# Mixer's front: ScalarE normalises the first chunk, VectorE evicts its turned blocks, TensorE multiplies the identity with itself 20 times beforehand

## The chip, the cores and the metric

The program runs on one core of one Trainium2 chip. The metric is device microseconds of one execution. The kernel before was timed three times: median 945.87 us, from 944.41 to 945.95 us.

## What is computed

The input is `x`, 2 sequences of 2048 tokens with 128 features. Four stages follow each other, each with a layer norm ahead of it and its result added to `x`: a Mamba mixer, a mixture of 8 experts, a linear attention, and the same mixture of experts again. The change is in the first stage alone:

```
xn = layernorm(x)                       # over the 128 features, eps 1e-5
x_m, z = split(xn @ W_in)               # 256 channels each
x_m = silu(conv(x_m, 4 taps) + conv_b)
dt_low, Bc, Cc = split(x_m @ W_x)
dt = softplus(dt_low @ W_dt + b_dt)
state[t] = exp(dt * A) * state[t-1] + dt * Bc * x_m     # 16 states a channel
y = (sum(state * Cc) + x_m * D) * silu(z)
x = x + y @ W_out
```

Then `x + moe(layernorm(x))`, `x + attention(layernorm(x))` and `x + moe(layernorm(x))`.

## The kernel before

Everything is float32. The mixer (`mamba`, from line 36) keeps the 4096 tokens in `X` as 32 tiles of 128 tokens by 128 features. Eight tiles are a chunk, so there are four chunks; four tiles fill a PSUM bank of 512 columns when they are turned.

Each engine has a program of its own, and semaphores order them. The front, which the change touches, goes like this for chunk 0:

- SyncE (lines 244 to 259) issues the four loads of `X`, then seven loads that count on one semaphore, `w_loaded`: `w_x`, `w_dt`, `w_out`, `decay_rate` and three small vectors into `chan`, `b_dt` last. ScalarE's queue issues three more weights (lines 328 to 331).
- VectorE takes the statistics of a chunk (`token_stats`, line 452, with lines 28, 31 and 457), ScalarE the square root (`std`, line 337), VectorE the reciprocal and the shift (lines 464 and 466), and then VectorE normalises the 8 tiles into `xn` (line 471). `xn` is a view of the tile `decay`, so the trace names it `decay`. The statistics of chunks 1 to 3 and the normalisation of their 24 tiles come behind that in VectorE's program.
- TensorE turns the tiles (`turn`, line 578; a bank is ready when `turned` counts), and ScalarE copies bank 0 and bank 1 into `xn_T` (`take_turned`, line 341), which counts on `xnT_ready`.
- GpSimd makes the convolution's weights meanwhile: `w_tap` (line 283, 4 multiplications), then the copy of `pick` into `pick_r` (line 286), then `skip` (line 290), which waits for all of `w_loaded`.
- TensorE then waits for `taps_ready`, for all of `w_loaded` (line 673) and for two banks of `xn_T` (line 682). Its pieces `u` (line 623) are four matmuls each, one for each tap, 512 columns wide. The order written out in `START` (line 209) is: two `u` pieces of the first half of the chunk, bank 2 turned (chunk 1's first four tiles), two `u` pieces of the second half, the `mixed` pieces (line 634), `bT`, `v`, then banks 3 to 7 turned, `again`. ScalarE evicts the `u` pieces with Silu (line 350) and bank 2 (line 341).

After the front there is a loop of 128 steps (16 states, 2 channel blocks, 4 chunks): ScalarE makes the decay (line 432), VectorE the drive (line 538) and the scan (line 555), GpSimd the product with C (line 323), TensorE sums the products (line 702). A step of the loop cannot begin before the front has made `dt` and `u` of chunk 0, and the stages behind the mixer begin when the loop has ended.

Of the kernel before, what the change touches and what calls it, by code (L numbers as in the profile page):

```python
# [16 lines left out]
ACT = mybir.ActivationFunctionType  # L17
ALU = mybir.AluOpType

P = 128  # L20
BANK = 512
# [3 lines left out]
def layer_norm_constants(dve, chain, at, stats, moments, source, tiles):  # L25

    for i in range(tiles):
        dve.bn_stats(stats[:, i, :], source(i)).then_inc(chain, 1)
    dve.wait_ge(chain, at + tiles)
    for i in range(tiles):  # L30
        dve.bn_aggr(moments[:, i, :], stats[:, i, :]).then_inc(chain, 1)
    dve.wait_ge(chain, at + 2 * tiles)
    return at + 2 * tiles

def mamba(nc, X, ident, x, W_in, conv_w, conv_b, A_log, D, W_x, W_dt, b_dt, W_out):

    BATCH, L, DM = x.shape
    KC, _, CH = conv_w.shape
    NS = A_log.shape[1]  # L40
    R = W_dt.shape[0]
# [4 lines left out]
    CT = CHUNK // P  # L46
    TB = CHUNK // BANK
    BT = BANK // P
    RING = 4
    CHUNKS = BATCH * NCHUNK  # L50
# [8 lines left out]
    with nc.cleanup_on_exit(), ExitStack() as ctx:  # L59
        def sb(name, shape, dt=F32):  # L60
            return ctx.enter_context(nc.sbuf_tensor(name, shape, dt))

        def sem(name):
            return nc.alloc_semaphore(name)

        psum = ctx.enter_context(nc.psum_tensor("m_psum", [P, 8, BANK], F32))
        Y, DRIVE, PIECE = 0, 2, 6
# [13 lines left out]
        rstd = sb("m_rstd", [P, BATCH * TILES])  # L81
        shift = sb("m_shift", [P, BATCH * TILES])
        xn_T = sb("xn_T", [P, BATCH * L])
# [19 lines left out]
        xn = decay[:].rearrange("p r (t d) -> p (r t) d", d=DM)  # L103
# [14 lines left out]
        dve_chain = sem("m_dve_chain")  # L118
        variance = sem("variance")
        std_done = sem("std_done")  # L120
        normed = sem("normed")
        turned = sem("turned")
        xnT_ready = sem("xnT_ready")
# [108 lines left out]
        def place(n):  # L232
            h, s = divmod(n, NS)
            return h // KB, h % KB, s
# [92 lines left out]
        def _(act):  # L327
# [5 lines left out]
            def std(first, end):  # L333

                act.wait_ge(variance, end)
                part = rstd[:, first * CT:end * CT]
                act.activation(part, part, ACT.Sqrt).then_inc(std_done, 1)

            def take_turned(g):
                act.wait_ge(turned, g + 1)  # L340
                act.copy(xn_T[:, g * BANK:(g + 1) * BANK], psum[:, g % 4, :]).then_inc(xnT_ready, 1)  # L341
# [63 lines left out]
                             psum[:, Y + t, :]).then_inc(y_taken, 1)  # L405

            std(0, 1)
            take_turned(0)
            take_turned(1)
            std(1, CHUNKS)  # L410
            act.wait_ge(w_loaded, 16 * 7)
            for number, piece in enumerate(START):
# [7 lines left out]
            for n in range(STEPS):  # L420
                g, k, s = place(n)
# [3 lines left out]
                if before >= 0:  # L425
                    act.wait_ge(scanned, before + 1)
                    was, was_k, was_s = place(before)
                    if starts_batch(was):
# [4 lines left out]
                               scale=decay_rate[:, k, s:s + 1]).then_inc(decay_ready, 1)  # L433
# [15 lines left out]
        def _(dve):  # L449
            at = 0  # L450

            def token_stats(g, at):
                dve.wait_ge(x_loaded[g], 16)
                tiles = slice(g * CT, (g + 1) * CT)
                at = layer_norm_constants(dve, dve_chain, at, stats[:, tiles, :], moments[:, tiles, :],
                                          lambda i: X[:, g * CT + i, :], CT)
                dve.tensor_scalar(rstd[:, tiles], moments[:, tiles, 1], LN_EPS, None,
                                  ALU.add).then_inc(variance, 1)
                return at

            def normalise(first, end, at):
                tiles = slice(first * CT, end * CT)
                dve.wait_ge(std_done, 2 if first else 1)
                dve.reciprocal(rstd[:, tiles], rstd[:, tiles]).then_inc(dve_chain, 1)
                dve.wait_ge(dve_chain, at + 1)
                dve.scalar_tensor_tensor(out=shift[:, tiles], in0=moments[:, tiles, 0], scalar=-1.0,
                                         in1=rstd[:, tiles], op0=ALU.mult,
                                         op1=ALU.mult).then_inc(dve_chain, 1)
                dve.wait_ge(dve_chain, at + 2)
                for i in range(first * CT, end * CT):  # L470
                    dve.tensor_scalar(xn[:, i, :], X[:, i, :], rstd[:, i:i + 1], shift[:, i:i + 1],
                                      ALU.mult, ALU.add).then_inc(normed, 1)
                return at + 2

            at = normalise(0, 1, token_stats(0, at))
            for g in range(1, CHUNKS):
                at = token_stats(g, at)
            at = normalise(1, CHUNKS, at)
            dve.wait_ge(w_loaded, 16 * 7)  # L480
            dve.wait_ge(constants, 1)
            for k in range(KB):
# [36 lines left out]
            for number, piece in enumerate(START):  # L519
                if piece[:4] == ("again", 0, 0, 0):  # L520
                    dve.wait_ge(rate_exp, 1)
                    dve.tensor_scalar(decay_rate[:], decay_rate[:], -1.0, None,
                                      ALU.mult).then_inc(rate_ready, 1)
                    for g in range(TB + 1, BATCH * L // BANK):
                        dve.wait_ge(turned, g + 1)
                        dve.tensor_copy(xn_T[:, g * BANK:(g + 1) * BANK],
                                        psum[:, g % 4, :]).then_inc(xnT_ready, 1)
                use(piece, number)
            dve.wait_ge(dt_ready, TB)
            dve.wait_ge(u_ready, KB * TB)  # L530
# [41 lines left out]
        def _(pe):  # L572
            def turn(g):
                if g >= 4:
                    pe.wait_ge(xnT_ready, g - 3)
                for i in range(4):
                    pe.wait_ge(normed, 4 * g + i + 1)
                    last = pe.transpose(psum[:, g % 4, i * P:(i + 1) * P], xn[:, 4 * g + i, :], ident[:])
                last.then_inc(turned, 1)
# [28 lines left out]
            def unit(piece, number, i):  # L608
# [51 lines left out]
                elif kind == "out":  # L660
# [6 lines left out]
                                             start=(c == 0), stop=(c == KB - 1))  # L667
                    last.then_inc(projected, 1)

            for g in range(TB):  # L670
                turn(g)
            pe.wait_ge(taps_ready, KC)
            pe.wait_ge(w_loaded, 16 * 7)
            for number, piece in enumerate(START):
                kind, _, k, t, _ = piece
                if (kind, k, t) == ("u", 0, 1):
                    turn(TB)
                if (kind, t) == ("again", 0):
                    for g in range(TB + 1, BATCH * L // BANK):
                        turn(g)  # L680
                if kind == "u":
                    pe.wait_ge(xnT_ready, t + 2)
                if kind == "mixed":
                    pe.wait_ge(w_all_ready, 1)
                    pe.wait_ge(constants, 5)
                for i in range(KC if kind == "u" else KB if kind == "mixed" else 1):
                    unit(piece, number, i)
# [21 lines left out]
            for n in range(STEPS + LAG):  # L709
                g, k, s = place(n)  # L710
                if n < STEPS:
# [4 lines left out]
                    if maker(n) == "dve":  # L716
                        for t in range(TB):
                            last = pe.matmul(pair(n)[:, t, :], pick_r[B_AT:P, s, :],  # L718
                                             b_split[B_AT:P, g % 2, t * BANK:(t + 1) * BANK],
                                             start=True, stop=True)  # L720
# [869 lines left out]
def build(nc, inputs, out):  # L1590

    mixer = {k[len("L0_attn_a_"):]: v for k, v in inputs.items() if k.startswith("L0_attn_a_")}
    linear = {k[len("L0_attn_b_"):]: v for k, v in inputs.items() if k.startswith("L0_attn_b_")}
    experts = {k[len("L0_ffn_"):]: v for k, v in inputs.items() if k.startswith("L0_ffn_")}
    BATCH, L, DM = mixer["x"].shape
    T = BATCH * L
    between = nc.dram_tensor("between", [T, DM], F32, kind="Internal").ap()
    with ExitStack() as ctx:
        X = ctx.enter_context(nc.sbuf_tensor("X", [P, T // P, DM], F32))
        ident = ctx.enter_context(nc.sbuf_tensor("ident", [P, P], F32))  # L1600
        identity(nc, ident)
        mamba(nc, X, ident, **mixer)

        E, FF, _ = experts["fc1s"].shape
        shared = {name: ctx.enter_context(nc.sbuf_tensor(f"shared_{name}", shape, F32))
                  for name, shape in (("gamma", [P, 2]), ("b1_T", [P, E * FF // P]),
                                      ("b2_all", [P, E, DM]), ("gate_pad", [P, P + P // E - 1]),
                                      ("w1_T", [P, E, FF]), ("w2_T", [P, E, FF // P, DM]))}
        moe(nc, X, ident, shared, "f1", between, True, **experts)
        attention(nc, X, ident, between, **linear)  # L1610
        moe(nc, X, ident, shared, "f2", out.rearrange("b l d -> (b l) d"), False, **experts)
# [26 lines left out]
```

## Time and profile before

| | us |
|---|---|
| median of three timed runs | 945.87 |
| lowest, highest | 944.41, 945.95 |
| span of the profiled execution, first to last instruction | 955.9 |
| VectorE busy, share of the span | 652.0, 68% |
| TensorE busy, share of the span | 683.2, 71% |

The profiled execution has a span that is 10.0 us longer than the median of the timed runs; of that execution no other time is known. So a stretch read from the trace is about one per cent longer than in a timed run, if what the profiler adds is spread evenly, which the trace doesn't tell. Times in the trace count from the first instruction. A group in the timeline is a run of instructions of one kind: its start, and the time from that start to the end of the last of them.

### The profile page before, as it was taken

Reading aid. Unit: us, or ns where it says so; the run is one execution under the profiler, and the core shown is the slowest. Engines: PE = TensorE matmul, PEld = TensorE weight load, DVE = VectorE, ACT = ScalarE, POOL = GpSimd, SP = SyncE. Lnnn points to the kernel's source line nnn. Section 1 sums busy time; section 2 is a strip of 40 time slices with the busy share of each in tenths; the row PEclk is TensorE's granted clock in tenths of the full one; section 3 lists DMA queues with packets and bytes.
Section 4 is the critical chain, followed back from the end, with each engine's and each line's share of the span. In section 5 each row is a group of like instructions: output and inputs, shape, how many; then the busy total and the mean of one; then the engine's idle time right before and its main releaser. Section 6 shows DMA issues by size and latency. Waiting matters only on the chain. (4 is left out here: it accounts for less than half of the span.)

```text
span 955.9 us, 11388 instructions
## 1 busy us (share of the span) xinstructions
PE 683.2 (71%) x3643; PEld 487.6 (51%) x3643; DVE 652.0 (68%) x1169; ACT 527.3 (55%) x987; POOL 529.8 (55%) x417
## 2 busy tenths in 40 slices
PE   4868987889887898988876575669550952277951
PEld 1445555665556655666655453546340841255631
DVE  6598889988898969899999598623112698832210
ACT  1569998579985989867984266023210446012320
POOL 5047657675667755576768330458861041176874
PEclk9978998889997899779889675589875876568976
DMA  5134343444344334443544360413334005122332
GB/s 134 62 117 149 134 137 134 152 135 132 133 136 154 134 132 137 149 135 133 171 139 132 94 194 13 110 35 41 41 29 102 1 1 154 31 53 30 42 34 22
DMA packets 59751, 95.55 MB, mean 100 GB/s; under 512 B 6344, under 2 KB 39920, under 8 KB 59696
## 3 DMA queue, kind: packets, MB, share of 16 engines
q1 hardware_dynamic: 47872, 85.15, 27.7%
q0 software_dynamic: 11264, 8.66, 7.2%
q10 hardware_dynamic: 560, 1.05, 0.4%
q8 instruction: 29, 0.48, 0.2%
q14 instruction: 26, 0.21, 0.1%
HBM read 81.73 MB, written 13.11 MB: 99 GB/s over the span
## 5 line engine op out<-in xcount | busy, mean ns | idle before, releaser
L323 POOL TENSOR_TENSOR product<-state,c_all 128x1024 f32<-128x1024 f32 x128 | 302.0, 2371 | 192.2 <-DVE state L555 177.9
L555 DVE TENSOR_TENSOR_SCAN state<-decay,m_psum 128x1024 f32<-128x1024 f32 x64 | 145.2, 2281 | 14.2 <-PE m_psum L728 5.6
L555 DVE TENSOR_TENSOR_SCAN state<-decay,carry,m_psum 128x1024 f32<-128x1024 f32 x64 | 148.7, 2340 | 7.5 <-PE m_psum L728 3.6
L702 PE MATMUL m_psum<-ident,product 128*128 128x128 f32 x1024 | 151.3, 296 | 3.3 <-POOL product L323 3.3
L1058 ACT ACTIVATE f_f_T<-f_psum,shared_b_T 128x512 f32<-128x512 f32 x64 | 44.0, 688 | 188.6 <-PE f_psum L1368 166.8
L432 ACT ACTIVATE decay<-dt,decay_rate 128x1024 f32<-128x1024 f32 x128 | 145.3, 1144 | 2.8 <-DVE state L555 2.4
L702 PEld LDWEIGHTS m_psum<-ident,product 128*128 128x128 f32 x1024 | 125.6, 153 | 33.8 <-issue 26.2
L389 ACT ACTIVATE drive_T<-dtu_T,b_T 128x128 f32<-128x128 f32 x384 | 121.7, 389 | 15.1 <-PE m_psum L728 13.7
L800 POOL DMA_INDIRECT f_got<-f_table,f_tokens x64 | 66.1, 1032 | 99.8 <-DMA f_table<-f_rows 41.4
L538 DVE TENSOR_TENSOR m_psum<-m_psum,dtu 128x1024 f32<-128x1024 f32 x80 | 97.3, 1217 | 26.4 <-PE m_psum L718 26.0
L718 PE MATMUL m_psum<-b_split,pick_r 64*128 64x512 f32 x160 | 64.2, 483 | 26.4 <-DVE state L555 26.1
L1353 PE MATMUL f_psum<-shared_w_T,f_f_T 128*128 128x128 f32 x512 | 66.9, 294 | 13.9 <-issue 7.5
L1353 PEld LDWEIGHTS f_psum<-shared_w_T,f_f_T 128*128 128x128 f32 x512 | 64.6, 208 | 19.3 <-issue 17.9
L1368 PE MATMUL f_psum<-f_y_T,shared_w_T 128*128 128x512 f32 x128 | 64.4, 650 | 7.9 <-DVE f_y_T L1224 7.9
L1224 DVE TENSOR_SCALAR f_y_T<-f_psum,shared_gamma 128x512 f32<-128x512 f32 x16 | 13.0, 810 | 81.9 <-PE f_psum L1342 65.3
L623 PE MATMUL m_psum<-xn_T,w_tap 128*128 128x512 f32 (+2 forms) x128 | 66.2, 647 | 1.6 <-ACT xn_T L341 1.6
L1000 POOL DMA_INDIRECT between<-f_f,f_tokens x32 | 50.4, 1576 | 21.4 <-issue 8.8
L1000 POOL DMA_INDIRECT out<-f_f,f_tokens x32 | 50.3, 1573 | 20.6 <-DVE f_f L1243 9.5
L728 PE MATMUL m_psum<-ident,drive_T 128*128 128x128 f32 x384 | 58.3, 302 | 3.7 <-DVE state L555 3.0
L728 PEld LDWEIGHTS m_psum<-ident,drive_T 128*128 128x128 f32 x384 | 50.5, 158 | 17.2 <-issue 9.7
L718 PEld LDWEIGHTS m_psum<-b_split,pick_r 64*128 64x128 f32 x160 | 26.0, 203 | 59.8 <-DVE state L555 39.4
L1236 DVE TENSOR_TENSOR f_f<-f_psum,shared_b_all 128x512 f32<-128x512 f32 x16 | 11.0, 690 | 57.4 <-PE f_psum L1353 57.4
(194 smaller groups left out, 1079.1 us busy)
## 6 DMA issues: line engine op xcount, KB each, us to landing
c_all<-c_dram SPq DMA_DIRECT2D x128, 512.0 KB, 3.7
f_table<-f_rows SPq DMA_DIRECT2D x2, 2176.0 KB, 9.6
X<-in_L_attn_a_x SPq DMA_DIRECT2D x4, 512.0 KB
f_w_raw<-in_L_ffn_fc2s SPq DMA_DIRECT2D x1, 2048.0 KB, 15.8
between<-f_f SPq DMA_DIRECT2D x1, 2048.0 KB, 8.7
X<-between SPq DMA_DIRECT2D x4, 512.0 KB
out<-f_f SPq DMA_DIRECT2D x1, 2048.0 KB, 8.7
f_got<-f_table,f_tokens POOLq DMA_INDIRECT x64
```

What stands on the lines that cost most here:

```text
L323: pool.tensor_tensor(product[:, n % RING, :], state[:, n % RING, :], c_all[:, n % RING, :], ALU.mult).then_inc(product_ready, 1)
L389: act.activation(drive_T[:, turn % 2, i], dtu_T[:, k, i], ACT.Copy, scale=b_T[:, g % 2, i, s:s + 1]).then_inc(act_drive, 1)
L432: act.activation(decay[:, n % RING, :], dt[:, k, :], ACT.Exp, scale=decay_rate[:, k, s:s + 1]).then_inc(decay_ready, 1)
L538: dve.tensor_tensor(pair(n), pair(n), dtu[:, k, :].rearrange("p (a t) -> p a t", t=BANK), ALU.mult).then_inc(drive_ready, 1)
L555: dve.tensor_tensor_scan(state[:, n % RING, :], decay[:, n % RING, :], pair(n).rearrange("p a t -> p (a t)"), 0.0 if starts_batch(g) else ...
L623: ins = pe.matmul(out[:, lo:hi], w_tap[:, j, k * P:(k + 1) * P], xn_T[:, first + lo:first + hi], start=(i == 0), stop=(i == KC - 1))
L702: last = pe.matmul(psum[:, Y + i // BT, i % BT * P:(i % BT + 1) * P], product[:, n % RING, i * P:(i + 1) * P], ident[:], start=False, stop ...
L718: last = pe.matmul(pair(n)[:, t, :], pick_r[B_AT:P, s, :], b_split[B_AT:P, g % 2, t * BANK:(t + 1) * BANK], start=True, stop=True)
L728: last = pe.transpose(pair(n)[:, i // BT, i % BT * P:(i % BT + 1) * P], drive_T[:, made(n, "act", "pool") % 2, i], ident[:])
L800: pool.indirect_dma_start(got[:, e, t, :], None, table, bass.IndirectOffsetOnAxis(ap=tokens[:, e, t:t + 1], axis=0)).then_inc(gathered[e], 16)
L1000: pool.indirect_dma_start(dst, bass.IndirectOffsetOnAxis(ap=tokens[:, e, t:t + 1], axis=0), o[:, e % AHEAD, t, :], None, compute_op=ALU.ad ...
L1353: last = pe.matmul(psum[:, OUT + r, t * DM:(t + 1) * DM], hidden[:, r, q, t * P:(t + 1) * P], w2_T[:, e, q, :], start=(q == 0), stop=(q == ...
```

## The change

ScalarE normalises chunk 0's eight tiles (Identity with a scale and a bias for each partition), as soon as VectorE has made `shift`; VectorE goes on with the statistics of chunk 1, copies banks 0 and 1 out of PSUM, and then takes the statistics of chunks 2 and 3. The wait between `shift` and VectorE's own 24 normalisations goes by a new semaphore, `ln_ready`. TensorE multiplies the identity with itself 20 times into a bank that isn't in use yet, before it waits for the first normalised tile.

```diff
+        ln_ready = sem("m_ln_ready")
@@ ScalarE
             std(0, 1)
-            take_turned(0)
-            take_turned(1)
+            act.wait_ge(ln_ready, 1)
+            for i in range(CT):
+                act.activation(xn[:, i, :], X[:, i, :], ACT.Identity, bias=shift[:, i:i + 1],
+                               scale=rstd[:, i:i + 1]).then_inc(normed, 1)
             std(1, CHUNKS)
@@ VectorE
-            def normalise(first, end, at):
+            def take_turned(g):
+                dve.wait_ge(turned, g + 1)
+                dve.tensor_copy(xn_T[:, g * BANK:(g + 1) * BANK], psum[:, g % 4, :]).then_inc(xnT_ready, 1)
+
+            def scale_and_shift(first, end, at):
                 tiles = slice(first * CT, end * CT)
                 dve.wait_ge(std_done, 2 if first else 1)
                 dve.reciprocal(rstd[:, tiles], rstd[:, tiles]).then_inc(dve_chain, 1)
                 dve.wait_ge(dve_chain, at + 1)
                 dve.scalar_tensor_tensor(out=shift[:, tiles], in0=moments[:, tiles, 0], scalar=-1.0,
                                          in1=rstd[:, tiles], op0=ALU.mult,
-                                         op1=ALU.mult).then_inc(dve_chain, 1)
-                dve.wait_ge(dve_chain, at + 2)
-                for i in range(first * CT, end * CT):
-                    dve.tensor_scalar(xn[:, i, :], X[:, i, :], rstd[:, i:i + 1], shift[:, i:i + 1],
-                                      ALU.mult, ALU.add).then_inc(normed, 1)
-                return at + 2
-
-
-            at = normalise(0, 1, token_stats(0, at))
-            for g in range(1, CHUNKS):
+                                         op1=ALU.mult).then_inc(ln_ready, 1)
+                return at + 1
+
+
+            at = scale_and_shift(0, 1, token_stats(0, at))
+            at = token_stats(1, at)
+            for g in range(TB):
+                take_turned(g)
+            for g in range(2, CHUNKS):
                 at = token_stats(g, at)
-            at = normalise(1, CHUNKS, at)
+            at = scale_and_shift(1, CHUNKS, at)
+            dve.wait_ge(ln_ready, 2)
+            for i in range(CT, CHUNKS * CT):
+                dve.tensor_scalar(xn[:, i, :], X[:, i, :], rstd[:, i:i + 1], shift[:, i:i + 1],
+                                  ALU.mult, ALU.add).then_inc(normed, 1)
@@ TensorE
+            WARM = 20
+            for i in range(WARM):
+                pe.matmul(psum[:, PIECE, 0:P], ident[:], ident[:], start=True, stop=True)
             for g in range(TB):
                 turn(g)
```

The copies of banks 3 to 7 on VectorE now call the new `take_turned`, with the same two instructions as before.

## Rows read from the trace of the kernel before

**Rows 1.** The page's costliest groups: count, busy us, mean ns, idle before, releaser.

```profile
L323 POOL TENSOR_TENSOR product<-state,c_all 128x1024 f32<-128x1024 f32 x128 | 302.0, 2371 | 192.2 <-DVE state L555 177.9
...
L555 DVE TENSOR_TENSOR_SCAN state<-decay,carry,m_psum 128x1024 f32<-128x1024 f32 x64 | 148.7, 2340 | 7.5 <-PE m_psum L728 3.6
```

**Rows 2.** Timeline, block's start and chunk 0: start, us, engine, line, operation, count, idle before.

```profile
2.01 0.31 POOL L272 MEMSET w_all<- 128x256 f32 x1 [0.48 <-POOLq L744]
...
9.74 0.17 DVE L466 SCALAR_TENSOR_TENSOR m_shift<-m_moments,m_rstd 128x8 f32<-128x8 f32 x1
9.94 5.41 DVE L471 TENSOR_SCALAR decay<-X,m_rstd,m_shift 128x128 f32<-128x128 f32 x8
...
10.40 2.78 POOL L283 TENSOR_TENSOR w_tap<-product 128x256 f32<-128x256 f32 x4 [2.03 <-DMA product<-in_L_attn_a_conv_w]
...
13.31 1.96 POOL L286 CAST pick_r<-state 64x2048 fp32r<-64x2048 f32 x1
...
15.92 0.59 ACT L341 COPY xn_T<-m_psum 128x512 f32<-128x512 f32 x1 [2.87 <-PE m_psum L578]
```

**Rows 3.** One line's instructions: ns min/median/max, first and last start.

```profile
L471 DVE TENSOR_SCALAR decay<-X,m_rstd,m_shift x32: 335/343/1910, 9.9 to 29.4; 128x128 f32<-128x128 f32 x32
```

**Rows 4.** Timeline: the last weight load's issue, and GpSimd's wait for it.

```profile
12.84 0.47 SPq L258 DMA_DIRECT2D chan<-in_L_attn_a_b_dt  x1
...
15.89 1.21 POOL L290 TENSOR_SCALAR skip<-ident,chan 128x128 f32<-128x128 f32 x2 [0.62 <-DMA chan<-in_L_attn_a_b_dt]
```

**Rows 5.** Timeline: the first two `u` pieces, their weight loads, the next eviction.

```profile
16.65 9.89 PE L623 MATMUL m_psum<-xn_T,w_tap 128*128 128x512 f32 x16 [0.77 <-ACT xn_T L341]
...
20.19 0.34 PEld L623 LDWEIGHTS m_psum<-xn_T,w_tap 128*128 128x128 f32 x1 [0.51 <-issue]
21.05 0.34 PEld L623 LDWEIGHTS m_psum<-xn_T,w_tap 128*128 128x128 f32 x1 [0.52 <-issue]
...
22.51 0.19 PEld L623 LDWEIGHTS m_psum<-xn_T,w_tap 128*128 128x128 f32 x1 [0.27 <-issue]
...
22.94 0.19 PEld L623 LDWEIGHTS m_psum<-xn_T,w_tap 128*128 128x128 f32 x1 [0.24 <-issue]
...
27.16 0.58 ACT L341 COPY xn_T<-m_psum 128x512 f32<-128x512 f32 x1
```

**Rows 6.** Timeline: the first scan of the loop.

```profile
52.47 2.29 DVE L555 TENSOR_TENSOR_SCAN state<-decay,m_psum 128x1024 f32<-128x1024 f32 x1
```

**Rows 7.** Timeline, first mixture of experts: Sqrt's table, then Identity on such tiles.

```profile
538.80 1.28 ACT L1012 ACT_TABLE_LOAD   x1 [8.23 <-PEq L59]
...
546.39 3.17 ACT L1026 ACTIVATE f_f<-X,f_shift,f_rstd 128x128 f32<-128x128 f32 x8
...
546.92 3.17 PE L1273 MATMUL f_psum<-ident,f_f 128*128 128x128 f32 x8 [1.78 <-ACT f_f L1026]
```

**Rows 8.** Timeline: VectorE's statistics of chunk 1, first and last group.

```profile
15.27 1.63 DVE L28 BATCH_NORM_STATS2 m_stats<-X 128x6 f32<-128x128 f32 x8
...
17.62 0.17 DVE L457 TENSOR_SCALAR m_rstd<-m_moments 128x8 f32<-128x8 f32 x1
```

**Rows 9.** Timeline: VectorE reading PSUM beside a busy GpSimd.

```profile
65.44 2.36 POOL L323 TENSOR_TENSOR product<-state,c_all 128x1024 f32<-128x1024 f32 x1 [1.15 <-DVE state L555]
...
67.30 1.40 DVE L500 TENSOR_SCALAR dt<-m_psum,chan 128x512 f32<-128x512 f32 x2
```

**Rows 10.** Timeline: eight float32 multiplications of 128 by 128, two records each.

```profile
59.47 3.78 PE L697 MATMUL m_psum<-skip,u 128*128 128x128 f32 x16
```

**Rows 11.** Timeline: an idle stretch of TensorE in the front.

```profile
51.17 1.07 PE L653 MATMUL m_psum<-ident,dtu 128*128 128x128 f32 x8 [2.27 <-DVE dtu L531]
```

**Rows 12.** Busy time of PE, PEld, DVE, ACT, POOL by stretch, then PEclk.

```profile
48.00:52.00 4.00, 1.73 (x13) 1.09 (x11) 3.60 (x4) 2.14 (x2) 0.00 (x0) 1.00 0.39 155
52.00:56.00 4.00, 2.09 (x7) 0.79 (x4) 3.79 (x4) 4.00 (x8) 1.07 (x1) 0.62 0.00 0
398.00:404.00 6.00, 6.00 (x22) 4.09 (x20) 4.40 (x4) 5.93 (x11) 4.67 (x2) 0.50 0.41 158
```

More of the change, by code:

```diff
@@ L524, in _ @@
                     for g in range(TB + 1, BATCH * L // BANK):
-                        dve.wait_ge(turned, g + 1)
-                        dve.tensor_copy(xn_T[:, g * BANK:(g + 1) * BANK],
-                                        psum[:, g % 4, :]).then_inc(xnT_ready, 1)
+                        take_turned(g)
                 use(piece, number)
```

## The prediction

> **What bounds the kernel now.** I read the page's groups first: the mixer's loop of 128 steps fills more than half of the span, with one product of 2.37 us on GpSimd and one scan of 2.34 us on VectorE in every step [rows 1]. The change doesn't touch a step of that loop. It touches the front, which is a single chain: no scan starts before the front has made `dt` and `u` of chunk 0, and the first one starts at 52.47 us [rows 6]. Whatever the front loses or gains on that chain is passed on once, to a kernel of 946 us. So the question is what ends last in the front, and I read the timeline there, step by step.
>
> VectorE has the shift at 9.91 us (9.74 and 0.17) and then needs 5.41 us for eight tiles [rows 2]. The same instruction takes 0.34 us as a rule and 1.91 at worst [rows 3]: the eight would need 2.7. The lost time lies beside GpSimd's `w_tap` (from 10.40) and its cast into `pick_r` (13.31 to 15.27); VectorE's last tile ends at 15.35, just behind the cast. Bank 1 is then turned and copied by ScalarE from 15.92 to 16.51 [rows 2], and the first `u` matmul starts 0.14 us later, at 16.65 [rows 5].
>
> The second view is the one that decides: GpSimd's `skip` waits for all of `w_loaded`, and goes on at 15.89, released by the load of `b_dt`, which SyncE had issued at 12.84 [rows 4]. TensorE has the same wait ahead of its first `u` piece (line 673). So if the tiles had come at once, `u` could have started only some 0.7 us earlier.
>
> Third, TensorE's own speed. The first sixteen `u` passes (two pieces, four taps, two records for each float32 matmul) take 9.89 us, from 16.65 to 26.54. Their weight loads stand 0.86 us apart at 20.19 and 21.05, and 0.43 apart at 22.51 and 22.94 [rows 5]: TensorE runs at 1.2 GHz for the first part and at 2.4 from about 22.2 us on, after 5.6 us of dense work. About 6.5 passes are at the lower level.
>
> **The change, part by part.**
>
> *ScalarE normalises.* In the experts' front eight such Identity instructions take 3.17 us from the first to the end of the last, and TensorE, turning them as they come, ends 0.53 us behind them (550.09 against 549.56) [rows 7]. From 9.95 that gives tile 4 at about 11.6, tile 8 at 13.1 and bank 1 turned at 13.65. Price below: none, since ScalarE did nothing here but wait. Price above: two table loads of 1.28 us [rows 7], if Identity needed another table than Sqrt and Sqrt had to come back. In those rows Sqrt's load is the only one ahead of Identity, so I take no load. ScalarE's second square root waits for VectorE's statistics in both kernels, and Silu of the first piece comes later than that.
>
> *VectorE's order.* Statistics of chunk 1 take 2.52 us (15.27 to 17.79) [rows 8], so from 9.95 to 12.5; bank 0 is turned by 12.1. An eviction out of PSUM takes about 0.70 us there: two in 1.40, the first of them beside a product of GpSimd that ends at 67.80, without being longer for it [rows 9]. So bank 0 is copied by 13.2 and bank 1 from 13.65 to 14.4. The waits that this adds on VectorE hold up the statistics of chunks 2 and 3 and the 24 normalisations. They move forward all the same, since 5.41 us of normalising leave VectorE ahead of them and only 1.4 us of copies come in. Who waits for them is bank 2, turned behind the sixteenth `u` pass, long after. If the copies were held up by the cast, as the normalisations were, bank 1 would be ready at 15.27 plus 0.70, 15.97, and `u` would start at 16.1.
>
> *The 20 multiplications.* The `skip` products on TensorE are eight float32 multiplications of this size; they are sixteen records and take 3.78 us, 0.236 each [rows 10]. Forty records are then 9.4 us at that pace, which is my upper end; half of it, 4.7 us, is the lower one. The block starts at 2.01 us [rows 2], so they end between 6.7 and 11.5. The first normalised tile is there at about 10.4. At worst TensorE starts 1.1 us late on the turning, with four tiles waiting, and has caught up before tile 8 at 13.1. They cost nothing on the chain.
>
> *What is late next.* Banks at 14.4, `w_tap` at 13.18 (10.40 and 2.78 [rows 2]), `w_loaded` at about 15.87. The loads end last, and nothing in the change moves SyncE's queue. `u` starts 0.14 us behind them, at 16.0: 0.65 us earlier than before.
>
> *Does the warm-up help the `u` passes?* Between bank 1 (13.65) and 16.0 TensorE has nothing to do for 2.35 us, and before that only eight turns, 0.40 us apart. The nearest row is the 2.27 us of idleness ahead of 51.17 [rows 11]: the stretch from 48 to 52 has a granted clock of 1.00, the next four microseconds 0.62 [rows 12], so the clock fell to 1.2 GHz soon after the work had come back, although TensorE had been denser before that gap than eight turns make it. I take the same here: what the multiplications earn is lost before or shortly after `u` begins, and as many passes run slowly as before. Bounds: at 2.4 GHz throughout, sixteen passes are 6.9 us and a tail of 0.16, ending at 23.05 in place of 26.54, a gain of 3.5 us; with the rise at the same moment as before (22.2), 7.2 slow and 8.8 fast passes end at 26.1, a gain of 0.4.
>
> The Trainium skill, in "TensorE: Matmul & The Clock Gate", section "Why this matters for your kernels", advises matmuls ahead of the work to be timed, so that it runs at the full clock, and warns against idle gaps between bursts. [...]
>
> The sum: from 16.65 to 16.0, 0.65 us in the profiled execution, whose span is 955.9 us. All that follows in the front (the bank copied at 27.16 [rows 5], the first scan at 52.47) waits for the passes, so the 0.65 is carried to the end. A timed run is about one per cent shorter; that changes 0.65 by nothing. 945.87 less 0.65 is 945.2.
>
> **The rivals.**
>
> *A: the clock is kept, or kept for longer.* If the turns count for enough, the clock stays at 2.4 GHz over the gap: 945.87 less 3.5 is 942.4. If it falls only some two microseconds into `u` and comes back earlier than before, the gain is about half of that, 944.1. For it: TensorE was at 1.00 still when the work came back at 51.17. Against it: the fall behind that gap. Chance 0.20.
>
> *B: the loads land earlier in a run that isn't profiled.* Then the banks limit, `u` starts at 14.4 plus 0.14, 14.55, and the gain is 2.1 us: 943.8. For it: 10 us of the profiled span are not in the timed runs. Against it: GpSimd's chain hangs on loads too, so the kernel before would gain by it as well. Chance 0.05.
>
> *C: the shift is used up.* ScalarE loads another table twice (2.6 us, banks at 17.0, start at 17.1, 0.5 us later than before), or the shift is lost on the way to the first scan: 945.9 to 946.3. Chance 0.07.
>
> *D, slower: the clock stays low over the passes.* Once it has fallen in the gap, dense work alone need not bring it back at once: from 398 to 404 us TensorE is busy throughout at 0.50 [rows 12]. Sixteen passes of 0.86 with their tail end at 30.1, 3.5 us later: 949.4. It decides from the eighth slow pass on, since an earlier start of 0.65 pays for one and a half more than the 6.5 of now. Against it: in the front of the kernel before the same passes brought the clock up from the lower level. Chance 0.04.
>
> **How the numbers follow.** The forecast, 945.2, has the chance 0.64, with a range of its own from 944.4 to 946.0. About 0.2% (1.9 us) is what a measurement of this kernel can tell from no change, so faster means below 944.0 and slower above 947.8. Three quarters of A (0.15), most of B (0.04) and a little of the forecast's edge (0.02) are faster, 0.21; D and an edge of C are slower, 0.05; the rest, 0.74, is the same. The range reaches down to A's full price, 942.4, and up past C's, to 946.6; D lies outside.
>
> **What would show it.** In the trace after: VectorE without tiles of 0.7 us and 1.9 us in the front; eight Identity instructions in 3.2 us; bank 1 copied near 14.4; the first `u` matmul near 16.0, just behind GpSimd's `skip`; weight loads 0.86 us apart in its first passes; the first scan near 51.8. Wrong would be: a `u` matmul well ahead of `skip`'s start (then line 673 doesn't decide), passes 0.43 us apart from the first on (A), or a first scan that hasn't moved (C).

## The result and the profile after

| | us | |
|---|---|---|
| forecast | 945.2 | 942.4 to 946.6 |
| kernel before, 14 runs, the three from before among them | 945.41 | 943.43 to 946.34 |
| changed kernel, 14 runs | 947.05 | 945.52 to 948.6 |

The ratio is 1.002, with a 95% interval from 1.0012 to 1.0028: about 1.6 us slower (947.05 less 945.41). That is under the 1.9 us at which the prediction drew its line, but it is a loss, beyond its interval, where a small gain had been forecast, and above the range.

The front goes through the steps that the prediction named. This is the timeline of the changed kernel (start, us to the end of the group, engine, line, operation, count, idle before); it answers to [rows 2, 5, 6 and 7]:

```profile
2.05 6.58 PE L680 MATMUL m_psum<-ident 128*128 128x128 f32 x40 [2.05 <-PEq L755]
...
9.75 3.19 ACT L411 ACTIVATE decay<-X,m_shift,m_rstd 128x128 f32<-128x128 f32 x8 [0.47 <-DVE m_shift L473]
...
13.50 0.69 DVE L466 COPY xn_T<-m_psum 128x512 f32<-128x512 f32 x1 [0.54 <-PE m_psum L586]
...
16.19 1.20 POOL L291 TENSOR_SCALAR skip<-ident,chan 128x128 f32<-128x128 f32 x2 [1.14 <-DMA chan<-in_L_attn_a_b_dt]
16.19 8.82 PE L631 MATMUL m_psum<-xn_T,w_tap 128*128 128x512 f32 x16 [2.73 <-DMA chan<-in_L_attn_a_b_dt]
...
18.03 0.34 PEld L631 LDWEIGHTS m_psum<-xn_T,w_tap 128*128 128x128 f32 x1 [0.52 <-issue]
...
18.88 0.33 PEld L631 LDWEIGHTS m_psum<-xn_T,w_tap 128*128 128x128 f32 x1 [0.52 <-issue]
...
20.12 0.19 PEld L631 LDWEIGHTS m_psum<-xn_T,w_tap 128*128 128x128 f32 x1 [0.24 <-issue]
20.55 0.19 PEld L631 LDWEIGHTS m_psum<-xn_T,w_tap 128*128 128x128 f32 x1 [0.24 <-issue]
...
52.53 2.29 DVE L563 TENSOR_TENSOR_SCAN state<-decay,m_psum 128x1024 f32<-128x1024 f32 x1
```

The 20 multiplications are 40 records and end at 8.63, ScalarE's eight Identity instructions take 3.19 us without a table load in between, VectorE has copied bank 1 by 14.19, although GpSimd's cast runs beside it (13.16 to 15.05), and the first `u` matmul starts in the same moment as GpSimd's `skip`, at 16.19, both released by the last load into `chan`. The weight loads are 0.85 us apart at 18.03 and 0.43 apart at 20.12: the passes begin at 1.2 GHz. The stretches show where the clock that the multiplications had earned went (columns as in [rows 12]):

```profile
4.00:8.00 4.00, 4.00 (x29) 4.00 (x29) 1.50 (x8) 1.04 (x1) 3.71 (x3) 1.00 1.07 303
8.00:12.00 4.00, 2.12 (x11) 1.14 (x9) 3.55 (x29) 2.46 (x7) 2.12 (x4) 1.00 1.12 324
12.00:16.00 4.00, 1.29 (x4) 0.46 (x3) 3.43 (x14) 0.94 (x3) 2.91 (x3) 0.60 0.73 135
16.00:20.00 4.00, 3.81 (x5) 1.70 (x6) 3.54 (x28) 0.22 (x1) 1.20 (x2) 0.54 0.00 0
```

Full at first, 0.60 from 12 to 16. The granted clock is either 1.00 or 0.50; a mean of 0.60 over four microseconds is 0.8 us at the full one, so it falls near 12.8, during the last turns (they end at 13.47), and it rises again only under the `u` passes. The first scan starts at 52.53 us; a second trace of the kernel before has it at 53.21. So there is a lead, and the loss must lie behind it. Where a trace stands against another at one moment says little here: at the last scan of the loop the changed kernel is 1.04 us behind (525.56 against 524.52), at the attention's first load 1.18 ahead, and the two traces of the kernel before are themselves 2.0 apart at that scan. What tells is the length of a stretch that comes out the same in every trace but some. Such a one stands where the attention begins, 670 us behind the first scan. First the timeline, then the DMA view of the stretch from 720 to 735 us (the last number is the median time from issue to landing):

```profile
722.43 5.26 SPq L1452 DMA_DIRECT2D X<-between  x4
...
729.85 3.19 DVE L28 BATCH_NORM_STATS2 a_stats<-X 128x6 f32<-128x128 f32 x16 [25.56 <-DMA X<-between]
```

```profile
q8 instruction: 1, 0.02, 0.6%
...
X<-between SPq DMA_DIRECT2D x4, 512.0 KB, 7.2
```

The same in the second trace of the kernel before:

```profile
723.61 3.85 SPq L1441 DMA_DIRECT2D X<-between  x4
...
729.52 3.19 DVE L28 BATCH_NORM_STATS2 a_stats<-X 128x6 f32<-128x128 f32 x16 [24.14 <-DMA X<-between]
```

```profile
X<-between SPq DMA_DIRECT2D x4, 512.0 KB, 6.0
```

The changed kernel issues the attention's loads of `X` at 722.43, 1.18 us ahead of the other, and takes its first statistics at 729.85, 0.33 us behind it. Between the first issue and the first statistics lie 7.42 us in place of 5.91, and the issue itself takes 5.26 in place of 3.85. 1.51 us are lost here, about what the whole change costs. The two executions traced don't show the whole cost themselves: their spans are 944.5 and 944.4 us. In the same stretch queue 8, which brings TensorE's instructions (the runs below show it), carries one packet of 16 KB, from 723.62 on, 1.2 us behind the first issue. In the second trace of the kernel before that packet comes at 742.26 (DMA view from 740 to 745 us):

```profile
q8 instruction: 1, 0.02, 1.3%
```

### The profile page after: what moved, and what is told of

It reads as the page before. It is cut to its first block and busy times, and to the rows that moved or that the text cites. A ratio compares the mean times of both kernels' runs of the same rounds, so it can differ in the third digit from the quotient of the medians.

```text
span 944.5 us, 11468 instructions
## 1 busy us (share of the span) xinstructions
PE 686.6 (73%) x3683; PEld 491.3 (52%) x3683; DVE 647.4 (69%) x1163; ACT 529.2 (56%) x993; POOL 529.6 (56%) x417
## 5 line engine op out<-in xcount | busy, mean ns | idle before, releaser
L1364 PE MATMUL f_psum<-shared_w_T,f_f_T 128*128 128x128 f32 x512 | 63.2, 284 | 7.8 <-ACT f_f_T L1069 7.8
L1364 PEld LDWEIGHTS f_psum<-shared_w_T,f_f_T 128*128 128x128 f32 x512 | 61.0, 199 | 13.0 <-issue 8.3
L1379 PE MATMUL f_psum<-f_y_T,shared_w_T 128*128 128x512 f32 x128 | 61.9, 629 | 1.8 <-DVE f_y_T L1235 1.8
L1011 POOL DMA_INDIRECT between<-f_f,f_tokens x32 | 50.5, 1577 | 14.1 <-issue 9.1
```

The lines of the kernel that those rows point to most:

```text
L1011: pool.indirect_dma_start(dst, bass.IndirectOffsetOnAxis(ap=tokens[:, e, t:t + 1], axis=0), o[:, e % AHEAD, t, :], None, compute_op=ALU.ad ...
L1364: last = pe.matmul(psum[:, OUT + r, t * DM:(t + 1) * DM], hidden[:, r, q, t * P:(t + 1) * P], w2_T[:, e, q, :], start=(q == 0), stop=(q == ...
```

## The experiments

Each kernel was timed over five rounds beside the kernel before on the same chip, 11 or 12 runs of each and 5 of early_warm30; ratios are against the kernel before, with the 95% interval.

**The kernel before once more.** No edit.

> The kernel before, unchanged, for a second trace and as the measure of the spread. All theories: ratio 1.000 within 0.1%, first scan near 52.5 us. What it is to tell: whether the moments at which the granted clock rises and falls in the front (22.3, 42.7, 46.1 us in the first trace) stand at the same places in another execution; if the clock's moments have no fixed relation to the program's start, they are moved by up to some microseconds.

Measured: ratio 1.0004 (0.9995 to 1.0014), span 944.4 us. Here are the lines of its front:

```profile
15.62 0.59 ACT L341 COPY xn_T<-m_psum 128x512 f32<-128x512 f32 x1 [2.87 <-PE m_psum L578]
15.73 1.21 POOL L290 TENSOR_SCALAR skip<-ident,chan 128x128 f32<-128x128 f32 x2 [0.76 <-DMA chan<-in_L_attn_a_b_dt]
...
16.35 9.28 PE L623 MATMUL m_psum<-xn_T,w_tap 128*128 128x512 f32 x16 [0.77 <-ACT xn_T L341]
...
19.89 0.34 PEld L623 LDWEIGHTS m_psum<-xn_T,w_tap 128*128 128x128 f32 x1 [0.51 <-issue]
20.75 0.19 PEld L623 LDWEIGHTS m_psum<-xn_T,w_tap 128*128 128x128 f32 x1 [0.52 <-issue]
...
53.21 2.29 DVE L555 TENSOR_TENSOR_SCAN state<-decay,m_psum 128x1024 f32<-128x1024 f32 x1
```

Two things follow. The clock's moments have no fixed place: the rise that stood near 22.2 us in the first trace [rows 5] stands 1.5 us earlier here, ahead of the weight load at 20.75. And bank 1 was ready 0.3 us earlier than in [rows 2], so `u` started at 16.35 and not at 16.65: half of the forecast lead was a property of one execution. The first trace's span, 11.5 us longer than this one, has its extra time behind the mixer; its last scan of the loop starts at 522.51 us, 2.0 ahead of this one's.

**The parts apart.** The changed kernel without its multiplications, and the kernel before with them alone:

```diff
-            WARM = 20
-            for i in range(WARM):
-                pe.matmul(psum[:, PIECE, 0:P], ident[:], ident[:], start=True, stop=True)
```

```diff
+            WARM = 20
+            for i in range(WARM):
+                pe.matmul(psum[:, PIECE, 0:P], ident[:], ident[:], start=True, stop=True)
             for g in range(TB):
                 turn(g)
```

> The change without the 20 multiplications of the identity; all the rest as changed. Theory W (the multiplications cost the 1.6 us, by where they leave TensorE's clock or its instruction stream): the time is that of the kernel before or up to 0.7 us below it, 944.7 to 945.5 us, ratio 0.999 to 1.000. Theory F (the new order of ScalarE's and VectorE's work costs it): 947.0 us, ratio 1.0017, as the whole change. In the trace of either the first u matmul stands near 16.0 to 16.2 us.

> The kernel before with the 20 multiplications alone; VectorE normalises and ScalarE evicts as before. Theory W: slower than before by 1.6 us or more, ratio 1.0017. Theory F: as before, ratio 1.000 within 0.1%. A third one, C (the first u passes run half in the slow clock whatever is done, and a lead is lost at the next fall of the clock): both this one and the change without multiplications give 1.000 within 0.1%, and the 1.6 us come from the two together.

Measured: without them 0.9998 (0.9988 to 1.0009), with them alone 1.0016 (1.0004 to 1.0029). The loss belongs to the multiplications, and theories F and C fall. The trace of the second one tells which way. In the mixer's loop it is level with the second trace of the kernel before, or ahead of it: the first scan at 53.25 against 53.21, the last one of the loop at 524.37 against 524.52. At the attention it is 1.5 us behind (first statistics at 731.03 against 729.52). What the multiplications do to the clock of the front cannot be the cause of a loss that begins at 723 us.

```diff
+            for i in range(160):
+                pe.wait_ge(constants, 1)
             for g in range(TB):
                 turn(g)
```

Measured: 1.0023 (1.001 to 1.0036), span 945.4 us. Timeline and DMA view where the attention begins:

```profile
723.72 5.26 SPq L1443 DMA_DIRECT2D X<-between  x4
...
731.11 3.19 DVE L28 BATCH_NORM_STATS2 a_stats<-X 128x6 f32<-128x128 f32 x16 [25.57 <-DMA X<-between]
```

```profile
q8 instruction: 1, 0.02, 0.8%
...
X<-between SPq DMA_DIRECT2D x4, 512.0 KB, 7.1
```

7.39 us between issue and statistics, and the packet of queue 8 among the loads: the signature of the changed kernel, without a multiplication. The waits lasted longer than expected, and TensorE took its first turn at 11.01 us in place of 10.05, but `u` started at 16.38, as in the second trace of the kernel before (16.35), so that isn't what was lost.

**Other numbers of multiplications.** In the changed kernel `WARM = 10` and `WARM = 30`, 40 and 120 instructions.

> The whole change with 10 multiplications in place of 20: 40 instructions. Theory I: the fetch falls near 739 us, behind the loads of X, and nothing is held up: 944.8 us as without the multiplications, ratio 0.9998, at most 1.0008. Theory K: about half of what 20 cost, 945.8 us, ratio 1.0008 to 1.0017.

> The whole change with 30 multiplications: 120 instructions. Theory I: the fetch falls near 701 us, ahead of the attention's loads, during the experts' last scatters: 944.8 us, ratio 0.9998, unless another block now meets another load (up to 1.0016). Theory K: more than with 20, 947 us or above, ratio 1.002.

Measured: 1.0000 (0.999 to 1.001) with 10, 0.9996 (0.9986 to 1.0005) with 30. Their attention, and the stretch in which queue 8's packet stands: with 10 from 730 to 742 us, with 30 from 699 to 704.

```profile
722.04 3.87 SPq L1452 DMA_DIRECT2D X<-between  x4
...
727.96 3.19 DVE L28 BATCH_NORM_STATS2 a_stats<-X 128x6 f32<-128x128 f32 x16 [24.07 <-DMA X<-between]
```

```profile
q8 instruction: 1, 0.02, 0.5%
```

```profile
723.11 3.86 SPq L1452 DMA_DIRECT2D X<-between  x4
...
729.02 3.19 DVE L28 BATCH_NORM_STATS2 a_stats<-X 128x6 f32<-128x128 f32 x16 [24.24 <-DMA X<-between]
```

```profile
q8 instruction: 1, 0.02, 1.1%
```

5.92 and 5.91 us. The cost is not proportional to the multiplications: none with 10, 1.5 us with 20, none with 30. It goes by where the packet falls: with 20 among the loads of `X`, with 10 behind them (736.37), with 30 ahead of them (700.46). Theory K falls.

**What holds the lead back.** The prediction said that the last weight load decides when `u` starts, and that the idle gap behind the turns costs the clock. Moving the seven weight loads in SyncE's program between the second and third load of `X` tests both:

```diff
-            for g in range(CHUNKS):
+            def load_x(g):
                 b, c = divmod(g, NCHUNK)
                 sp.dma_start(X[:, g * CT:(g + 1) * CT, :],
...
+            load_x(0)
+            load_x(1)
             for out, source in ((w_x[:], W_x.rearrange("(k p) n -> p k n", p=P)),
...
                     sp.dma_start(chan[:, n, :], source.rearrange("(k p) -> p k", p=P)
                                  ).then_inc(w_loaded, 16)
+            load_x(2)
+            load_x(3)
```

> The kernel before, with SyncE's seven weight loads moved between the second and the third load of X; nothing else. Theory L (in the changed kernel the last weight load decides when the u passes start): here bank 1 decides, copied by ScalarE at 16.2 to 16.5 us, so the time is as before, ratio 0.999 to 1.000. Theory N (the weights' moment doesn't matter, TensorE is held by something else): the same here.

> The change without the multiplications, with the same weights moved forward. Theory L: the first u matmul moves from 16.0 to about 14.4 us, where bank 1 is ready, and the lead reaches the end in part, 1 to 2 us: 943.0 us, ratio 0.998 to 0.999. Theory N: u still near 16 us and ratio 1.000.

> The whole change with 30 multiplications (whose blocks are fetched elsewhere than with 20) and the weights moved forward. Theory L: u from 14.4 us. TensorE then waits less than 1 us between the turns and u; if the short gap is what decides, the u passes run 0.43 us apart from the start, end near 21.5 us, and 2 to 4 us are gained, 941 to 943 us, ratio 0.996 to 0.998. If the turns alone let the clock fall, it is as without multiplications, ratio 0.998 to 0.999.

Measured: in the kernel before 0.9999 (0.9989 to 1.0009); in the change without multiplications 0.9980 (0.9971 to 0.9989), 942.93 us; in the change with 30 of them 0.9953 (0.9939 to 0.9966), 939.39 us against 944.60. The last one beats the kernel before by 5.2 us, more than was expected; the change itself was not timed beside it. TensorE's timeline, without and then with them:

```profile
10.20 3.17 PE L591 MATMUL m_psum<-ident,decay 128*128 128x128 f32 x8 [10.20 <-ACT decay L416]
14.24 9.03 PE L636 MATMUL m_psum<-xn_T,w_tap 128*128 128x512 f32 x16 [0.88 <-DVE xn_T L471]
```

```profile
11.30 1.94 PE L591 MATMUL m_psum<-ident,decay 128*128 128x128 f32 x8
14.12 7.10 PE L636 MATMUL m_psum<-xn_T,w_tap 128*128 128x512 f32 x16 [0.88 <-DVE xn_T L471]
```

In both `u` starts some 2 us earlier than in the changed kernel, 0.88 us behind the last turn, released by bank 1's copy and no longer by the loads. Without the multiplications the sixteen passes take 9.03 us, with them 7.10. The granted clock of the second says why, from 6 to 22 us:

```profile
6.00:10.00 4.00, 4.00 (x33) 4.00 (x32) 3.18 (x22) 0.53 (x2) 2.23 (x2) 1.00 1.12 334
10.00:14.00 4.00, 3.08 (x22) 2.22 (x20) 3.67 (x19) 2.86 (x8) 3.56 (x5) 1.00 1.25 242
14.00:18.00 4.00, 3.88 (x9) 1.81 (x10) 3.90 (x26) 0.00 (x0) 2.32 (x3) 1.00 0.14 35
18.00:22.00 4.00, 3.66 (x12) 1.64 (x10) 3.61 (x21) 2.93 (x5) 0.00 (x0) 1.00 0.00 0
```

At 1.00 throughout. The first scan starts at 47.20, in the version without multiplications at 50.81. Of these 3.61 us, 2.05 are there when the sixteenth pass ends (21.22 against 23.27). The rest arises behind it, where the clock has another dip: from 42 to 46 us it was granted 1.00 with the multiplications and 0.57 without. That dip also differed between the two traces of the kernel before (0.98 and 0.74 from 46 to 50 us), so this part is not shown to come from the multiplications, though the timed runs have the whole difference, 3.5 us.

The kernel warm30 has the same 30 multiplications with the weights late. Its `u` passes, and its clock from 12 to 20 us:

```profile
16.35 7.94 PE L631 MATMUL m_psum<-xn_T,w_tap 128*128 128x512 f32 x14 [2.95 <-DMA chan<-in_L_attn_a_b_dt]
```

```profile
12.00:16.00 4.00, 1.23 (x4) 0.47 (x4) 3.54 (x16) 1.02 (x3) 3.00 (x3) 1.00 0.73 140
16.00:20.00 4.00, 3.65 (x5) 1.64 (x6) 3.54 (x27) 0.22 (x1) 1.20 (x2) 0.59 0.00 0
```

The clock outlasts the turns there too, but behind an idle stretch of 2.95 us it falls as soon as `u` has begun, and the first scan, at 52.72, is only 0.23 us ahead of that without multiplications (52.95).

**Ten and twenty with the weights early.** The same kernel with `WARM = 10` and `WARM = 20`.

> The change with 10 multiplications and the weights moved forward. Theory L with the gap deciding: the multiplications end near 6.2 us, four microseconds ahead of the first turn, so the clock falls before the u passes and the time is that of the version without multiplications, 942.9 us, ratio 0.998. If any multiplications at the start are enough: as with 30, 939.4 us, ratio 0.995.

> The change as it is, 20 multiplications, with the weights moved forward. Theory I (blocks) with theory L: the front as with 30 if the clock outlasts the turns, but the block fetched among the attention's loads of X costs its 1.5 us again: 940.9 us, ratio 0.997; if the clock falls during the turns, as it did in the trace of the changed kernel, 944.4 us, ratio 0.9995.

Measured: 0.9979 (0.997 to 0.9989) with 10, 0.9994 (0.9984 to 1.0005) with 20. The clock in both, from 6 and from 10 us on:

```profile
6.00:10.00 4.00, 0.35 (x4) 0.16 (x2) 3.26 (x22) 0.60 (x2) 2.22 (x2) 0.91 1.11 338
10.00:14.00 4.00, 3.17 (x8) 1.46 (x8) 3.44 (x18) 2.79 (x8) 3.71 (x5) 0.50 1.23 245
14.00:18.00 4.00, 3.81 (x5) 1.78 (x6) 3.93 (x26) 0.00 (x0) 2.17 (x3) 0.50 0.11 27
```

```profile
10.00:14.00 4.00, 2.63 (x8) 1.11 (x8) 3.56 (x18) 2.80 (x8) 3.73 (x5) 0.93 1.25 241
14.00:18.00 4.00, 3.94 (x5) 1.85 (x6) 3.90 (x26) 0.00 (x0) 2.15 (x3) 0.50 0.14 33
```

With 10, the last multiplication ends 3.8 us ahead of the first turn (6.35 and 10.15), and the clock is down from 10 us on. With 20 it ends 1.25 us ahead of it (8.91 and 10.16), and the clock is down from 14 on, as in the changed kernel, although TensorE waits only 0.88 us between turns and `u`; only with 30, which reach to 11.47 and into the turns, did it stay. With 20 the packet of queue 8 also stands among the attention's loads again:

```profile
719.59 5.33 SPq L1457 DMA_DIRECT2D X<-between  x4
...
727.04 3.19 DVE L28 BATCH_NORM_STATS2 a_stats<-X 128x6 f32<-128x128 f32 x16 [25.59 <-DMA X<-between]
```

7.45 us. So this kernel has both faults of the change at once: of the two per mille that the early weights bring without multiplications, about half a one is left.

## Why the prediction was wrong

*ScalarE's normalising, VectorE's evictions and order:* right. Bank 1 was forecast for 14.4 and stood at 14.19; no table load, no copy held up by the cast.

*What is late next:* right. `u` starts with `skip`, on the last weight load, and moves to 14.1 when the weights are moved (early_warm30), while the kernel before gains nothing by the same move.

*The shift of 0.65 us:* mis-sized, by about half or more. It compared a start worked out from one execution with the latest of the starts before; the second trace gives 16.35, the change without multiplications 16.02 and the change itself 16.19, a lead of 0.33 or 0.16. The first scan of the first pair is 0.26 us apart. A gain of that size is inside the interval of the runs.

*Does the warm-up help the passes?* Right in the result, but not for the reason given. The passes began at 1.2 GHz. But the clock had fallen near 12.8 us, during the turns and ahead of the idle gap before `u`, so the row of the 2.27 us gap told the outcome by luck; with 20 multiplications a gap of 0.88 us didn't save it either. Where 30 multiplications carry the clock through the turns, the gap does decide (warm30 and early_warm30). The advice of the Trainium skill, "TensorE: Matmul & The Clock Gate", section "Why this matters for your kernels", to warm up first and to avoid idle gaps between bursts, agrees with that pair: 30 multiplications are worth about 3.6 us at the first scan (50.81 against 47.20) where the gap is 0.88 us, and 0.2 where it is 2.95.

*"They cost nothing on the chain":* this is the step that failed. It priced the 20 multiplications by TensorE's time and by who waits for TensorE in the front. They also lengthen TensorE's program by 80 instructions, and the program is itself a load. The block that is fetched at 742 us in the kernel before is fetched at about 724 in the changed one, when SyncE has just issued the attention's loads of `X`, for which the attention's whole front waits. The packet takes 1.45 us. Each of the loads counts sixteen arrivals, and the first statistics wait for two loads. Of the first load's arrivals, fifteen are there by 726.41 and the last at 727.95; of the second's, fifteen by 728.21 and the last at 729.75, and the statistics start at 729.85. In the second trace of the kernel before all sixteen of the first are there from 727.26 to 727.61, of the second from 729.07 to 729.42, and the statistics start at 729.52. The Trainium skill, "Runtime: NRT & Kernel Launch", section "Instruction fetch mechanics", has the blocks of 16 KiB for 256 instructions and calls the cost of a block's end mostly hidden. The packets of queue 8 agree on the size; here the cost of one of them fell on another engine's loads, and was not hidden. The prediction read no DMA queue but those of the data, though the profile's page listed queue 8 with 29 packets.

*The rivals.* A's gain exists, but it needs the loads out of the way and 30 multiplications in place of 20; C and D did not happen, and nothing shows B. The rival that did was not on the list: every rival lay in the front, and the loss lies at 723 us.

That one of the 16 DMA engines is held by this packet, and not by something that comes with it, rests on when it stands there: the four kernels with 80 more instructions have it among the loads, 1.1 to 1.2 us behind the first issue, one arrival of the second load is 1.5 to 1.6 us behind the other fifteen, and the stretch takes 7.35 to 7.45 us; the nine traces with none, 40 or 120 more haven't, and it takes 5.9. The packet's own time was 1.38 to 2.25 us in the four, so the delay isn't simply that time.

What remains open is the exact sum: from the first statistics to the end the four take 214.3 to 214.6 us and the others 214.8 to 215.3 (but for the first trace of the kernel before), so about 0.5 of the 1.5 us is won back in the traces, for a cause that no run shows, while the timed loss is 1.6, with an interval from 1.1 to 2.6. Open is also whether the clock's fall under 20 multiplications with early weights, and not under 30, is the same in every execution: each has one trace.

## To carry to other kernels

An instruction costs more than its time on its engine: it moves the rest of that engine's program, and the blocks in which the program is fetched can land among loads that somebody waits for. Where a small edit at the start of a long program gives a loss of a microsecond or two, look at the far end for a load that lands late on one engine, and try the same edit with another number of instructions before judging it (here 40 or 120 in place of 80). Work that is only to keep TensorE's clock up paid here only where it reached into the turns ahead of the work that it was for; first take away what makes that work wait.

## What the runs showed of the hardware

Where a fetch of 16 KB of TensorE's instructions fell among four loads of 512 KB, one of the sixteen arrivals of a load came 1.5 us behind the others, the first use came 7.4 in place of 5.9 us behind the first issue, and issuing the four took 5.2 to 5.3 us in place of about 3.85. A PSUM eviction on VectorE, 128 by 512, took 0.69 us beside a cast on GpSimd, beside which a normalisation out of SBUF had taken 1.91. And the first rise of TensorE's clock differed by 1.5 us between two executions of one program.
